# A two-layer gated cross-attention kernel: loops written out, and the attention tail through queries by heads

## The chip, the core and the metric

The kernel runs on one core of one Trainium2 chip. The metric is the device time in microseconds of one execution, as the median of several. TensorE is called PE here (PEld for its weight loads), VectorE DVE, ScalarE ACT, GpSimd POOL, SyncE SP.

## The reference

Eight sequences of 100 tokens with 128 features pass two layers. Each layer has a gated cross-attention over 1444 context tokens of the same sequence, and a gated mixture of experts. Everything is float32. Cut to what matters here:

```python
# x (8, 100, 128), ctx (8, 1444, 128); 16 heads of 8
q = (layernorm(x) @ Wq + bq).reshape(B, S, H, D).transpose(0, 2, 1, 3)      # k, v the same from ctx
scores = einsum('bhqd,bhkd->bhqk', q, k) / sqrt(D)      # layer 0: where(mask, scores, lowest)
attention = softmax(scores, axis=-1)                    # layer 1: then times a gate of each key
out = einsum('bhqk,bhkd->bhqd', attention, v).transpose(0, 2, 1, 3).reshape(B, S, 128)
x = x + tanh(g_xattn[l]) * (out @ Wo + bo)
x = x + tanh(g_ffn[l]) * experts(layernorm(x))          # 64 experts + a shared one; 8 experts of 352
```

## The kernel before

The program is written per engine, and the order of each engine's instructions is fixed by hand; semaphores join the engines. It runs attention(0), experts(0), attention(1), experts(1) on all of them.

**Attention.** The eight sequences are the batches b. A batch is worked in 12 slots t, one for each tile of 121 keys. In slot t PE computes the scores of that tile for all 16 heads in four matmuls (g = 0 to 3) of 128x400, L1156 (in layer 0 each followed by the mask's matmul L1159); ACT takes the exponent of two groups at a time, L851; PE weighs the values with the exponents of the tile before, 16 small matmuls for each half, L1177, into the bank `po`. The rows of `po` are 32 to a head of a group (8 weighted values, then the sum of the exponents, then unused ones), its columns 4 groups by 100 queries.

Beside this, the slots of batch b prepare batch b + 1: its keys (L1086), its values (L1103), its queries stacked by head (POOL), and the maximum of the scores over all keys, which is to be subtracted. For that PE multiplies queries with keys in blocks ("chunks", L1129; 48 a batch in layer 0, 39 in layer 1), and DVE reduces each to one column (L417 with the mask in layer 0, L420 in layer 1). `MAX_PER_SLOT` tells how many chunks fall in a slot, and the constants `SCORES_TIME` to `TURN_TIME` after which of PE's steps in the slot each is issued. A chunk may not start before DVE has taken the one two before. At a batch's end DVE makes the row maxima (L427, L430), PE turns them (L1137), and DVE writes them into the stacked queries (L438), for which the next batch's scores wait.

**The tail of a batch** turns `po` into the attention's output. It lies in the slots of the following batch. In slot 0 ACT copies `po` to `oraw` (L879). In slot 3 (`DEN_SLOT`) PE spreads each head's sum over its 32 rows with the constant `den_sel` (`den`, L1195). In slots 3, 4, 5 and 6 DVE takes the reciprocal of one group of 100 columns each (`reciprocals`, L448), and behind the last multiplies `oraw` by them (`normalise`, L453). In slot 7 (`OUT_SLOT`) PE projects (`project`, L1201): four matmuls, one for each group, with a `wo` whose rows are spread to match (128 x 4 x 128, 256 KB a layer). Then DVE adds the bias, applies the gate and adds to the residual (`add_out`, L458, L461, L465). All of PE's results of the tail, and those for keys and values, share one bank, `pc`. The tail of batch 7 has no slots to lie in: it follows the stage, its four reciprocals one behind the other. Before it, the tail of batch 6 lies in the slots of batch 7, where DVE also normalises the tokens of batches 0 to 5 for the experts (`layer_norm`), splits them (`split_tokens`) and, in layer 0, begins the routing (`route0`).

**Loops.** Batches 1 to 6 are a hardware loop on each engine, three passes of two batches (SP has a similar one); batches 0 and 7 are written out. Inside, the batch number is in a register: thresholds of waits and some addresses are worked out from it.

**Experts.** 33 units of weights in layer 0 and 22 in layer 1. For each unit PE runs 12 matmuls (gate and up, `gate_up`) and 6 (down, `down`), all in L1294; ACT, DVE and POOL work between them (L928, L537, L775, L938, L528). Most units are in loops, four to a pass. At the end PE turns the sum with eight transposes (L1343).

## Time and profile before

| | us |
|---|---|
| median of 3 runs | 1180.16 |
| lowest, highest | 1178.17, 1180.94 |
| the profiled execution | 1175.95 |
| its span, first to last instruction | 1174.2 |

| engine | busy us | share |
|---|---|---|
| PE | 1022.6 | 87% |
| PEld | 715.6 | 61% |
| DVE | 853.9 | 73% |
| ACT | 543.2 | 46% |
| POOL | 349.4 | 30% |

The granted clock of TensorE averages 0.911 of full speed. The attention of layer 0 takes the span to about 500 us, its experts to 655, the attention of layer 1 to about 1040, its experts the rest. The rows quoted below come from the profiled page and from questions to the trace of the same execution. "issue" is time in which an engine waited for nothing that the profile shows. A letter q behind an engine's name is its sequencer.

### The profile page before, as it was taken

How to read it: one execution, taken by the hardware profiler on the slowest of the kernel's cores; microseconds unless marked ns; L12 is line 12 of the kernel's file. 1: busy time of each engine (PE TensorE's matmuls, PEld its weight loads, DVE VectorE, ACT ScalarE, POOL GpSimd, SP SyncE). 2: the span in 40 equal slices, each digit the busy share in tenths (PEclk: the TensorE clock that was granted, in tenths of full speed). 3: DMA queues.
4: the chain of work that ended last, by engine and by line, in shares of the span. 5: the costliest groups of instructions: out<-in, count | busy, mean ns of one | idle time of the engine just before them, and what ended most of it. 6: DMA issues, size and time to landing. Idle time of an engine off the chain costs nothing.

```text
span 1174.2 us, 27964 instructions
## 1 busy us (share of the span) xinstructions
PE 1022.6 (87%) x9788; PEld 715.6 (61%) x9788; DVE 853.9 (73%) x1943; ACT 543.2 (46%) x810; POOL 349.4 (30%) x278
## 2 busy tenths in 40 slices
PE   4889999799979999958999689999899899861997
PEld 2356666566656666647888446666566566541886
DVE  7977777667767776667999787778678578540896
ACT  2033534343434445625666315555555455640664
POOL 6522121212121201005777441242142241000674
PEclk8589999999989999968999959999899899975899
DMA  7531303030303040008554323414304304004662
GB/s 182 98 68 36 77 27 78 28 77 27 77 28 77 2 104 1 2 11 235 165 166 137 66 77 81 99 31 100 78 27 91 80 11 104 3 1 66 180 166 69
DMA packets 48235, 89.05 MB, mean 76 GB/s; under 512 B 21170, under 2 KB 31446, under 8 KB 48118
## 3 DMA queue, kind: packets, MB, share of 16 engines
q1 hardware_dynamic: 48118, 87.42, 30.6%
q8 instruction: 82, 1.34, 0.5%
q14 instruction: 35, 0.29, 0.1%
HBM read 47.70 MB, written 1.75 MB: 42 GB/s over the span
## 4 chain that ended last, share of the span: by engine, by line
PE 71%; DVE 12%; issue 8%; ACT 2%; POOL 1%; DVEq 0%; ACTq 0%; POOLq 0%
PE pm L1129 16%; PE po L1177 14%; PE ps L1156 12%; PE ps L1294 8%; PE ps L1159 6%; PE pm L1294 4%; PE pc L1086 4%; PE pc L1103 3%; DVE mx_part L420 2%; DVE qsel L528 2%; DVE negm L430 2%; PE pc L1201 1%; PE pc L1195 1%; DVE qst L438 1%; POOL tmpf L775 1%
## 5 line engine op out<-in xcount | busy, mean ns | idle before, releaser
L851 ACT ACTIVATE probs<-ps 121x800 f32<-121x800 f32 (+1 forms) x384 | 321.3, 838 | 339.9 <-PE ps L1159 216.3
L1129 PE MATMUL pm<-khi,qbd 128*100 128x482 f32 (+5 forms) x653 | 317.9, 498 | 12.8 <-DVE mx_part L417 9.7
L417 DVE CUSTOM_DVE_ANT_0 junk<-pm,negq 100x482 bf16<-100x482 f32 (+1 forms) x360 | 229.5, 654 | 76.4 <-PE pm L1129 58.8
L1156 PE MATMUL ps<-qst,kst 128*121 128x400 f32 (+1 forms) x768 | 263.8, 409 | 19.7 <-issue 13.8
L420 DVE TENSOR_REDUCE mx_part<-pm 128x1 f32<-128x482 f32 (+3 forms) x293 | 183.6, 650 | 49.7 <-PE pm L1129 49.6
L1177 PE MATMUL po<-probs,vaug 121*32 121x100 f32 x6144 | 216.0, 259 | 3.9 <-ACT oraw L879 3.6
L1177 PEld LDWEIGHTS po<-probs,vaug 121*32 121x32 f32 x6144 | 129.8, 111 | 118.3 <-issue 105.0
L1156 PEld LDWEIGHTS ps<-qst,kst 128*121 128x121 f32 (+1 forms) x768 | 142.3, 189 | 60.6 <-issue 40.9
L1129 PEld LDWEIGHTS pm<-khi,qbd 128*100 128x100 f32 (+2 forms) x653 | 115.2, 178 | 89.2 <-issue 36.6
L1294 PE MATMUL ps<-qsel,qst 128*128 128x400 f32 x660 | 140.6, 365 | 1.1 <-DVE qst L520 1.1
L775 POOL TENSOR_TENSOR tmpf<-vaug,wb 128x400 f32<-128x400 f32 x55 | 67.1, 1220 | 220.3 <-DMA wb<-routing 160.6
L1159 PE MATMUL ps<-negT,ident_b 121*121 121x400 bf16 (+1 forms) x384 | 132.2, 344 | 0.0
L1294 PEld LDWEIGHTS ps<-qsel,qst 128*128 128x128 f32 x660 | 129.5, 202 | 3.2 <-DVE qsel L572 1.4
L1294 PE MATMUL pm<-qsel,qst 128*128 128x400 f32 x330 | 84.4, 369 | 37.2 <-DVE qsel L528 34.0
L718 POOL TENSOR_TENSOR vaug<-vraw,bv 121x512 f32<-121x512 f32 x24 | 31.8, 1328 | 269.4 <-ACT vraw L872 269.4
L528 DVE TENSOR_TENSOR qsel<-tmpf,qsel 128x400 fp32r<-128x400 f32 x55 | 60.8, 1105 | 50.3 <-ACT qsel L938 50.3
L1294 PEld LDWEIGHTS pm<-qsel,qst 128*128 128x128 f32 x330 | 58.0, 193 | 55.7 <-DVE qsel L528 55.2
L718 POOL TENSOR_TENSOR vraw<-vraw,bv 121x512 f32<-121x512 f32 x24 | 31.1, 1298 | 190.7 <-ACT vraw L872 190.7
L702 POOL TENSOR_TENSOR qst<-qsel,head_mask 96x400 fp32r<-96x400 f32 x64 | 52.5, 850 | 85.2 <-PE po L1177 73.9
L775 POOL TENSOR_TENSOR t<-vaug,wb 128x400 f32<-128x400 f32 x55 | 72.9, 1325 | 0.5 <-DVE vaug L537 0.5
L938 ACT CAST qsel<-tmpf 128x400 fp32r<-128x400 f32 x55 | 29.0, 527 | 88.8 <-POOL tmpf L775 88.8
L402 DVE SCALAR_TENSOR_TENSOR klo<-pc,bk,khi 128x482 fp32r<-128x482 f32 (+1 forms) x42 | 30.0, 714 | 55.0 <-ACT khi L863 55.0
(176 smaller groups left out, 1109.8 us busy)
## 6 DMA issues: line engine op xcount, KB each, us to landing
kst<-khi SPq DMA_DIRECT2D x128, 180.5 KB, 3.8
wb<-routing SPq DMA_DIRECT2D x66, 200.0 KB, 3.5
ctxT<-in_ctxT SPq DMA_DIRECT2D x16, 722.0 KB, 4.4
kst<-klo SPq DMA_DIRECT2D x64, 180.5 KB, 3.9
wts<-in_experts SPq DMA_DIRECT2D x55, 192.0 KB, 3.4
wb<-routing SPq DMA_DIRECT2D x22, 400.0 KB, 4.0
qsel<-qhi SPq DMA_DIRECT2D x16, 100.0 KB, 2.4
routing<-vaug SPq DMA_DIRECT2D x1, 1100.0 KB
```

The costliest lines, as they stand in the source:

```text
L417: ins = nc.vector.tensor_tensor_reduce(junk[:, k % 2, 0:w], max_bank(b, k)[0:S, 0:w], negq[:, lo:lo + w], 1.0, -3e38, ALU.add, ALU.max, mx ...
L420: ins = nc.vector.tensor_reduce(mx_part[0:rows, i, c:c + 1], max_bank(b, k)[0:rows, 0:w], AX, ALU.max)
L528: nc.vector.tensor_tensor(h_lo[v], hw[v], h_hi[v], ALU.subtract).then_inc(m["h_low"], 1)
L702: nc.gpsimd.tensor_tensor(qst[par][0:96, g * GQ:(g + 1) * GQ].rearrange("p (j q) -> p j q", q=S), qsel[0:96, g, bass.ds(b * S, S)].unsquee ...
L718: nc.gpsimd.tensor_tensor(raw4 if l else dst, raw4, bias, ALU.add).then_inc(s["v_written"], 1)
L775: nc.gpsimd.tensor_tensor(hw[v], tu[v], wb[slot][:, v * HALF:(v + 1) * HALF], ALU.mult).then_inc(m["weighted"], 1)
L851: nc.scalar.activation(probs[t % 2][0:r, 2 * u * GQ:2 * (u + 1) * GQ].rearrange("p (g q) -> p g q", q=GQ), ps[0:r, 2 * u:2 * u + 2, 0:GQ], ...
L1129: nc.tensor.matmul(max_bank(b, k)[0:rows, 0:w], qbd[:, first:first + rows], khi[:, lo:lo + w], start=True, stop=True).then_inc(s["chunk_re ...
L1156: mm = nc.tensor.matmul(ps[0:r, g, 0:GQ], kst[par][:, g, t * KEY_TILE:t * KEY_TILE + r], qst[par][:, g * GQ:(g + 1) * GQ], start=True, sto ...
L1159: mm = nc.tensor.matmul(ps[0:r, g, 0:GQ].rearrange("p (j q) -> p j q", q=S), ident_b[0:r, 0:r], negT[0:r, t, :].unsqueeze(1).broadcast_to( ...
L1177: mm = nc.tensor.matmul(po[32 * j:32 * j + 32, g * S:(g + 1) * S], vaug[par][0:r, t, 9 * h:9 * h + 32], probs[t % 2][0:r, h * S:(h + 1) * ...
L1294: mm = nc.tensor.matmul(dst, w, x, start=(alone and k == 0), stop=(alone and k == 2), skip_group_check=not alone)
```

## The change

Two things are changed together.

1. Every hardware loop, on all five engines and in attention and experts, becomes a loop of the program that builds the kernel, so that its passes are written out one behind the other with constants in place of registers. They are DVE L495 and L552, POOL L760 and L780, ACT L908 and L953, PE L1278 and L1328, SP L1458 and L1510, all changed in the same way; the diff shows some of them.
2. The tail. In slot 3 PE turns `oraw` with four transposes, so that `pc` has the queries as rows and, as columns, 16 heads of 32. DVE then takes one reciprocal of 100x16 and multiplies, which gives 100x128 (`normalise`, both in slot 3). In slot 5 (`BACK_SLOT`) PE turns that back (`turn_back`) and DVE copies it out (`take_back`). In slot 7 PE projects with one matmul against the plain 128x128 `wo`. `den_sel` is no longer loaded, and `wo` has 64 KB a layer. The constants that place the chunks follow. On DVE, behind `layer_norm` of the stage's end, `take_back(6)` stands between `normalise(6)` and `split_tokens`.

```diff
@@ -77,14 +77,13 @@
 V_SLOTS = [8, 9, 10]
 
 
-DEN_SLOT, OUT_SLOT = 3, 7
-RECIPROCAL_SLOTS = {3: [0], 4: [1], 5: [2], 6: [3]}
+DEN_SLOT, BACK_SLOT, OUT_SLOT = 3, 5, 7
 
 
 BESIDE_AFTER = {1: 1, 2: 1, DEN_SLOT: 2}
 
 
-SCORES_TIME, WEIGH_TIME, K_TIME, V_TIME, DEN_TIME, OUT_TIME, TURN_TIME = (34, 17), 30, 80, 100, 67, 100, 10
+SCORES_TIME, WEIGH_TIME, K_TIME, V_TIME, DEN_TIME, BACK_TIME, OUT_TIME, TURN_TIME = (34, 17), 30, 80, 100, 40, 10, 25, 10
 
 
 NEGM_WRITES = [[(J * g, J * g + J, S) for g in range(G)], [(0, 4, 128), (4, 7, 128), (7, 10, 128), (10, 12, 128),
...
@@ -92,8 +91,8 @@
 
 IN_FLIGHT, IN_FLIGHT_FIRST = 2, 4
 
-TAIL = G + 3
-OUT_TAKEN = G + 1
+TAIL = 4
+OUT_TAKEN = 2
 
 
 PARTS = {"a": (0, 6), "b": (6, 8)}
...
@@ -152,7 +150,7 @@
         wq = [sb(f"wq{l}", [128, 128]) for l in range(2)]
         wk = [sb(f"wk{l}", [128, 128]) for l in range(2)]
         wv = [sb(f"wv{l}", [128, 128]) for l in range(2)]
-        wo = [sb(f"wo{l}", [128, G, 128]) for l in range(2)]
+        wo = [sb(f"wo{l}", [128, 128]) for l in range(2)]
         bq = [sb(f"bq{l}", [128, 1]) for l in range(2)]
         bk = [sb(f"bk{l}", [128, 1]) for l in range(2)]
         bv = [sb(f"bv{l}", [128, 128]) for l in range(2)]
...
@@ -199,8 +197,9 @@
         junk = sb("junk", [100, 2, 512], BF16)
         probs = [sb(f"probs{i}", [KEY_TILE, HQ]) for i in range(2)]
         oraw = sb("oraw", [128, GQ])
-        rden = sb("rden", [128, GQ])
-        onorm = sb("onorm", [128, GQ])
+        rden = sb("rden", [100, H])
+        onorm = sb("onorm", [100, D])
+        onormT = sb("onormT", [128, S])
 
 
         tmpf = sb("tmpf", [128, NKP])
...
@@ -441,20 +440,24 @@
                                                 max_mask[96:128, lo:hi].unsqueeze(2).broadcast_to([32, hi - lo, w]),
                                                 ALU.mult).then_inc(s["negm_ready"], 1)
 
-                def reciprocals(b, g):
-                    cols = slice(g * S, (g + 1) * S)
-
-                    dve.wait_ge(s["tail_ready"], 2 * b + 1)
-                    nc.vector.reciprocal(rden[:, cols], pc[:, cols]).then_inc(s["tail_step"], 1)
-
                 def normalise(b):
-                    dve.wait_ge(s["tail_step"], b * TAIL + G)
-                    dve.wait_ge(s["oraw_ready"], b + 1)
-                    nc.vector.tensor_tensor(onorm[:], oraw[:], rden[:], ALU.mult).then_inc(s["onorm_ready"], 1)
+
+                    turned = pc[0:S, :].rearrange("q (h e) -> q h e", e=32)
+                    dve.wait_ge(s["tail_ready"], 3 * b + 1)
+                    nc.vector.reciprocal(rden[:].unsqueeze(2), turned[:, :, DH:DH + 1]).then_inc(s["tail_step"], 1)
+                    dve.wait_ge(s["tail_step"], b * TAIL + 1)
+                    nc.vector.tensor_tensor(onorm[:].rearrange("q (h d) -> q h d", d=DH), turned[:, :, 0:DH],
+                                            rden[:].unsqueeze(2).broadcast_to([S, H, DH]), ALU.mult)\
+                        .then_inc(s["onorm_ready"], 1)
+
+                def take_back(b):
+
+                    dve.wait_ge(s["tail_ready"], 3 * b + 2)
+                    nc.vector.tensor_copy(onormT[:], pc[:, 0:S]).then_inc(s["onormT_ready"], 1)
 
                 def add_out(b):
 
-                    dve.wait_ge(s["tail_ready"], 2 * b + 2)
+                    dve.wait_ge(s["tail_ready"], 3 * b + 3)
                     nc.vector.tensor_tensor(t2[0:S, 0:D], pc[0:S, 0:D], bo[l][0:S, :], ALU.add)\
                         .then_inc(s["tail_step"], 1)
                     dve.wait_ge(s["tail_step"], b * TAIL + OUT_TAKEN)
...
@@ -469,9 +472,10 @@
 
                     if main and 0 < t < 3:
                         k_low(b + 1, t)
-                    if tail:
-                        for g in RECIPROCAL_SLOTS.get(t, []):
-                            reciprocals(b - 1, g)
+                    if tail and t == DEN_SLOT:
+                        normalise(b - 1)
+                    if tail and t == BACK_SLOT:
+                        take_back(b - 1)
 
                 def slots(b, main, tail, par):
 
...
@@ -482,8 +486,6 @@
                             chunk_max(b + 1, k)
                             if i == BESIDE_AFTER.get(t, 0):
                                 beside(b, t, main, tail)
-                            if tail and t == max(RECIPROCAL_SLOTS) and i == 1:
-                                normalise(b - 1)
                         if tail and t == OUT_SLOT:
                             add_out(b - 1)
                     row_max(b + 1, 1 - par)
...
@@ -492,14 +494,13 @@
                 slots(0, True, False, 0)
                 if l == 0:
                     energy_gates()
-                with dve.Fori(0, (B - 2) // 2) as i:
+                for i in range((B - 2) // 2):
                     for k in range(2):
                         slots(i * 2 + (1 + k), True, True, 1 - k)
 
                 layer_norm(2 * l + 1, "a")
-                for g in range(G):
-                    reciprocals(B - 2, g)
                 normalise(B - 2)
+                take_back(B - 2)
 
                 dve.wait_ge(s["vproj_done"], V_CHUNKS * B)
                 dve.wait_ge(s["qstack_ready"], G * B)
...
@@ -508,9 +509,8 @@
                 if l == 0:
                     route0("a")
                 add_out(B - 2)
-                for g in range(G):
-                    reciprocals(B - 1, g)
                 normalise(B - 1)
+                take_back(B - 1)
                 add_out(B - 1)
                 dve.wait_ge(s["tail_step"], TAIL * B)
 
...
@@ -757,7 +757,7 @@
                     nc.gpsimd.tensor_tensor(negT[:], negT[:], any_b[0:KEY_TILE, :].unsqueeze(1)
                                             .broadcast_to([KEY_TILE, KEY_TILES, S]), ALU.mult).then_inc(pool_init, 1)
                 prep(1, 1)
-                with pool.Fori(0, (B - 2) // 2) as i:
+                for i in range((B - 2) // 2):
                     for k in range(2):
                         prep(i * 2 + (2 + k), k)
 
...
@@ -1192,15 +1192,18 @@
                     else:
                         pe.wait_ge(s["negm_ready"], (b + 2) * len(NEGM_WRITES[l]))
                     pe.wait_ge(s["oraw_ready"], b + 1)
-                    nc.tensor.matmul(pc[:, 0:GQ], den_sel[:], oraw[:], start=True, stop=True)\
+                    for g in range(G):
+                        mm = nc.tensor.transpose(pc[0:S, g * 128:(g + 1) * 128], oraw[:, g * S:(g + 1) * S], ident[:])
+                    mm.then_inc(s["tail_ready"], 1)
+
+                def turn_back(b):
+                    pe.wait_ge(s["onorm_ready"], b + 1)
+                    nc.tensor.transpose(pc[:, 0:S], onorm[:], ident[0:S, 0:S]).then_inc(s["tail_ready"], 1)
+
+                def project(b):
+                    pe.wait_ge(s["onormT_ready"], b + 1)
+                    nc.tensor.matmul(pc[0:S, 0:D], onormT[:], wo[l][:], start=True, stop=True)\
                         .then_inc(s["tail_ready"], 1)
-
-                def project(b):
-                    pe.wait_ge(s["onorm_ready"], b + 1)
-                    for g in range(G):
-                        mm = nc.tensor.matmul(pc[0:S, 0:D], onorm[:, g * S:(g + 1) * S], wo[l][:, g, :],
-                                              start=(g == 0), stop=(g == G - 1))
-                    mm.then_inc(s["tail_ready"], 1)
 
                 def slots(b, main, after, prep, par):
 
...
@@ -1248,6 +1252,9 @@
                         if spreads:
                             den(b - 1, prep)
                             maxima(DEN_TIME)
+                        if turns_back:
+                            turn_back(b - 1)
+                            maxima(BACK_TIME)
                         if projects_out:
                             project(b - 1)
                             maxima(OUT_TIME)
...
@@ -1275,13 +1282,14 @@
 
                 slots(-1, False, False, True, 1)
                 slots(0, True, False, True, 0)
-                with pe.Fori(0, (B - 2) // 2) as i:
+                for i in range((B - 2) // 2):
                     for k in range(2):
                         slots(i * 2 + (1 + k), True, True, True, 1 - k)
                 slots(B - 1, True, True, False, 1)
                 for u in range(2):
                     weigh(B - 1, KEY_TILES - 1, u, 1)
                 den(B - 1, False)
+                turn_back(B - 1)
                 project(B - 1)
 
             def experts(l, opening=False):
...
@@ -1556,9 +1563,7 @@
             w = {n: m.T for n, m in w.items()}
         b = {n: i[f"L{l}_xattn_b{n}"] for n in "qkvo"}
         a[f"wq{l}"], a[f"wk{l}"], a[f"wv{l}"] = w["q"], w["k"], w["v"]
-        wo = np.zeros((J, 32, G, D), f)
-        wo[:, 0:DH] = w["o"].reshape(G, J, DH, D).transpose(1, 2, 0, 3)
-        a[f"wo{l}"] = wo.reshape(128, G, D)
+        a[f"wo{l}"] = w["o"]
         a[f"bq{l}"], a[f"bk{l}"] = b["q"][:, None], b["k"][:, None]
         a[f"bv{l}"], a[f"bo{l}"] = np.broadcast_to(b["v"], (128, 128)), np.broadcast_to(b["o"], (128, 128))
     a["wr0"], a["wr1"] = i["L0_ffn_gate_weight"].T, i["L1_ffn_router_w"].T
```

## Rows read from the trace of the kernel before

**Rows 1.** The page, section 4: the chain that ended last, by engine.

```profile
PE 71%; DVE 12%; issue 8%; ACT 2%; POOL 1%; DVEq 0%; ACTq 0%; POOLq 0%
```

**Rows 2.** Stretches from L1137 to L1137: length, busy (instructions) by engine, PEclk, DMA.

```profile
171.28:228.20 56.92, 54.05 (x569) 35.74 (x569) 40.59 (x113) 24.11 (x31) 10.00 (x8) 0.94 0.23 54
228.20:288.60 60.40, 54.29 (x569) 35.74 (x569) 40.42 (x113) 24.22 (x31) 9.99 (x8) 0.92 0.22 51
288.60:344.19 55.59, 52.70 (x569) 34.91 (x570) 40.57 (x113) 24.12 (x31) 10.01 (x8) 0.97 0.23 55
344.19:404.52 60.33, 54.34 (x569) 35.85 (x569) 40.42 (x113) 24.23 (x31) 10.00 (x8) 0.92 0.18 39
404.52:456.80 52.28, 51.15 (x569) 34.23 (x570) 38.83 (x113) 23.85 (x31) 7.12 (x7) 1.00 0.25 59
820.85:868.12 47.27, 42.46 (x513) 28.09 (x513) 32.82 (x57) 23.94 (x31) 13.08 (x12) 0.93 0.27 62
868.12:910.82 42.70, 40.88 (x513) 27.29 (x513) 32.92 (x57) 23.95 (x31) 13.07 (x12) 1.00 0.30 72
910.82:958.75 47.93, 43.12 (x513) 28.45 (x513) 32.82 (x57) 24.13 (x31) 13.08 (x12) 0.93 0.23 49
```

**Rows 3.** The chain that ended last, 228 to 236 us: start, length, what.

```profile
230.72 2.70 issue
```

**Rows 4.** Waits of PE: for what, us in total, times, longest.

```profile
PE ps L1156 <- issue: 13.8, 4, 3.9
```

**Rows 5.** The chain again, 600 to 620 us, layer 0's experts.

```profile
602.57 2.21 PE ps L1294 x12
...
617.10 2.20 PE ps L1294 x12
```

**Rows 6.** Stretches: slots 3, 7 of batch 0; 3, 4-6, 7 of batch 4.

```profile
77.66:81.24 3.58, 3.58 (x45) 2.41 (x44) 2.87 (x9) 1.83 (x3) 0.00 (x0) 1.00 0.71 155
92.06:96.14 4.08, 4.07 (x46) 2.54 (x45) 3.25 (x11) 1.67 (x2) 0.00 (x0) 1.00 0.00 0
304.33:308.63 4.30, 4.30 (x47) 2.81 (x46) 3.14 (x11) 1.67 (x3) 0.00 (x0) 1.00 0.73 150
308.63:319.46 10.83, 10.83 (x133) 7.24 (x132) 9.63 (x28) 5.19 (x7) 0.00 (x0) 1.00 0.68 147
319.46:324.48 5.02, 5.00 (x54) 3.44 (x53) 3.64 (x12) 1.68 (x2) 0.00 (x0) 1.00 0.00 2
```

**Rows 7.** The chain over the span: L1195 and L1201 in both layers.

```profile
305.90 0.87 PE pc L1195 x2
321.11 1.05 PE pc L1201 x8
...
942.16 0.87 PE pc L1201 x8
```

**Rows 8.** The chain over the span: transposes behind the experts.

```profile
653.81 1.08 PE ps L1343 x8
```

**Rows 9.** DVE in order of time: start, length, what, tiles, shapes.

```profile
496.79 0.29 DVE L458 TENSOR_TENSOR t<-pc,bo 100x128 f32<-100x128 f32 x1
```

**Rows 10.** Stretches of the last tail of each layer, columns as in rows 2.

```profile
498.00:504.37 6.37, 2.94 (x10) 1.96 (x10) 3.27 (x5) 1.16 (x1) 0.00 (x0) 0.82 0.01 3
1036.61:1042.57 5.96, 2.52 (x10) 1.54 (x10) 3.27 (x6) 1.16 (x1) 0.00 (x0) 0.90 0.00 0
```

**Rows 11.** Line L1343: ns least/median/most, first and last start.

```profile
L1343 PE MATMUL ps<-ident,vaug x16: 272/272/316, 653.8 to 1168.5; 128*100 128x128 f32 x16
```

**Rows 12.** Groups of DVE: busy us, mean ns | idle before, releaser.

```profile
L448 DVE RECIPROCAL rden<-pc 128x100 f32<-128x100 f32 x64 | 48.0, 765 | 21.2 <-PE pc L1195 21.2
...
L458 DVE TENSOR_TENSOR t<-pc,bo 100x128 f32<-100x128 f32 x16 | 4.6, 285 | 9.1 <-PE pc L1201 9.0
```

**Rows 13.** Line L604 alone, columns as in rows 11.

```profile
L604 DVE RECIPROCAL rsum<-rsum x1: 202/202/202, 518.6 to 518.6; 100x8 f32<-100x8 f32 x1
```

**Rows 14.** The page, section 3: a DMA queue, packets, MB, share.

```profile
q8 instruction: 82, 1.34, 0.5%
```

More of the change, by code:

```diff
@@ L114 @@
 CONSTS_EARLY = ["wk0", "bk0", "wv0", "ident", "wq0", "bq0", "head16_mask"]
-CONSTS_LATE = ["head_mask", "bv0", "max_mask", "den_sel", "gates", "wo0", "bo0", "before", "tie_mask", "wr0", "ebias",
+CONSTS_LATE = ["head_mask", "bv0", "max_mask", "gates", "wo0", "bo0", "before", "tie_mask", "wr0", "ebias",
                "wk1", "bk1", "wv1", "wq1", "bq1", "bv1", "wo1", "bo1", "wr1"]
@@ L142, in flamingo @@
         max_mask = sb("max_mask", [128, H])
-        den_sel = sb("den_sel", [128, 128])
         before = sb("before", [100, S])
@@ L281, in flamingo @@
             "khi_ready", "klo_ready", "vraw_ready", "v_written", "qstack_ready", "qbd_ready", "negm_ready",
-            "maxrow_ready", "kproj_done", "vproj_done", "onorm_ready", "tail_step", "rowmax_step", "chunk_seen")) for l in range(2)]
+            "maxrow_ready", "kproj_done", "vproj_done", "onorm_ready", "onormT_ready", "tail_step", "rowmax_step", "chunk_seen")) for l in range(2)]
         for l in range(2):
@@ L551, in experts @@
                 unit(1, 1)
-                with dve.Fori(0, (units - 4) // RING) as i:
+                for i in range((units - 4) // RING):
                     for k in range(RING):
@@ L779, in experts @@
                 weigh(0, 0)
-                with pool.Fori(0, (units - 1) // RING) as i:
+                for i in range((units - 1) // RING):
                     for k in range(RING):
@@ L907, in attention @@
                     step(nc.scalar.activation(egate[:], egate[:], ACT.Exp, scale=-1.0), "energy_exp")
-                with act.Fori(0, (B - 2) // 2) as i:
+                for i in range((B - 2) // 2):
                     for k in range(2):
@@ L952, in experts @@
                 unit(1, 1)
-                with act.Fori(0, (units - 4) // RING) as i:
+                for i in range((units - 4) // RING):
                     for k in range(RING):
@@ L1212, in slots @@
                         spreads = after and t == DEN_SLOT
+                        turns_back = after and t == BACK_SLOT
                         projects_out = after and t == OUT_SLOT
@@ L1215, in slots @@
                         whole = (main * G * SCORES_TIME[l] + weighs * 2 * WEIGH_TIME + projects_k * K_TIME
-                                 + projects_v * V_TIME + spreads * DEN_TIME + projects_out * OUT_TIME
+                                 + projects_v * V_TIME + spreads * DEN_TIME + turns_back * BACK_TIME + projects_out * OUT_TIME
                                  + turns_maxima * TURN_TIME)
@@ L1277, in attention @@
                 slots(0, True, False, True, 0)
-                with pe.Fori(0, (B - 2) // 2) as i:
+                for i in range((B - 2) // 2):
                     for k in range(2):
@@ L1327, in experts @@
                                      skip_group_check=True)
-                with pe.Fori(0, (units - 1) // RING) as i:
+                for i in range((units - 1) // RING):
                     for k in range(RING):
@@ L1415, in stack @@
                                      part[32 * g:32 * g + 32, :].bitcast(F32)).then_inc(s["kstack_in"][par], 16)
-            tile_of = dict(ident=ident, head_mask=head_mask, head16_mask=head16_mask, max_mask=max_mask, den_sel=den_sel,
+            tile_of = dict(ident=ident, head_mask=head_mask, head16_mask=head16_mask, max_mask=max_mask,
                            before=before, tie_mask=tie_mask, gates=gates, wr0=wr0, wr1=wr1, ebias=ebias)
@@ L1457, in attention @@
                 context(l, 3, 1)
-                with sp.Fori(0, (B - 4) // 2) as i:
+                for i in range((B - 4) // 2):
                     for k in range(2):
@@ L1509, in experts @@
                     context(1, 1, 1)
-                with sp.Fori(0, (units - RING) // RING) as i:
+                for i in range((units - RING) // RING):
                     for k in range(RING):
@@ L1546 @@
     a["max_mask"] = (row[:, None] - 96 == np.arange(H)).astype(f)
-    a["den_sel"] = (row[:, None] == row // 32 * 32 + DH).astype(f)
     a["before"] = (row[:S, None] < row[:S]).astype(f)
```

## Prediction, on record before the kernel ran

> **What bounds the kernel now.** First I read the chain that ended last, by engine: PE holds 71% of it, DVE 12% [rows 1]. So what is taken off DVE alone is worth nothing in most stretches, and what is taken off PE, or lets PE start again earlier, is worth its full length. Next, the attention stages batch by batch, cut where PE turns the row maxima (L1137), the last step of a batch's preparation [rows 2]. In layer 0 the stretches take 56.92, 60.40, 55.59, 60.33 and 52.28 us, in layer 1 47.27, 42.70 and 47.93. The reader is to see a pattern of two: the long ones lie where a loop body of two batches ends and jumps back (two such jumps in each layer, since each loop runs three times; its last pass falls through). Their granted clock is lower too (0.92 against 0.97; 0.93 against 1.00).
>
> The chain at one of these jumps shows what happens [rows 3]: DVE writes the last negated maxima until 230.72, and then nothing that the profile knows of holds PE back, yet its next matmul starts only 2.70 us later, "issue". The waits of PE list exactly four such stalls before L1156, 13.8 us, the longest 3.9 [rows 4]. At the other batch ends L1156 has none. The experts' loops jump back too, but there the chain keeps its step: from 602.57 to 617.10 are four units, 3.63 us each, which is one whole pass and so holds one jump [rows 5]. Their body is much shorter (36 PE instructions a unit by the code; an attention batch has over a thousand, weight loads counted [rows 2]).
>
> **Loops written out.** The same work is issued in the same order; the jumps, the counters and the register arithmetic for waits and addresses go. In layer 0 I compare 60.40 and 60.33 with 55.59: 4.8 + 4.7 = 9.5 us. In layer 1 47.27 and 47.93 with 42.70: 4.6 + 5.2 = 9.8 us. That is more than the bare stalls, because matmuls behind a stall run at 1.2 GHz for a while; in layer 1 the other batch ends show no fall of the clock at all [rows 2]. Sum 19.3 us. The bounds come from the neighbours: against 56.92, the worst ordinary stretch, layer 0 gives 6.9 instead of 9.5; against 52.28, plus some 1.7 us that its end lacks (there GpSimd prepares no further batch), 12.7. So 16.7 to 22.5. In the experts' loops: 0 [rows 5]. For the register arithmetic 0 as well: slots of batch 0, which is already written out, and of batches inside the loop differ only where the tail has work [rows 6].
>
> **The tail inside the stream (slots 3 to 7 of the following batch).** PE now spends 0.87 us on the denominators (two passes of 400 columns) and 1.05 us on the projection (four matmuls, eight instructions), 0.87 in layer 1, where I take 0.87 for the denominators too [rows 7]. The slots confirm it: slot 3 takes 4.30 us with the denominators and 3.58 without, slot 7 5.02 with the projection and 4.08 without [rows 6], so 0.72 + 0.94 = 1.66 of the 1.92 reach the slot lengths; the rest lies in slack that the slots have anyhow. Added are four transposes with 128 moving columns, one transpose back with 128, and one matmul of the projection's old form. Eight such transposes at the end of an expert stage take 1.08 us, so 0.135 each [rows 8]. New: 4 x 0.135 + 0.135 + 1.05/4 = 0.94 us, in layer 1 0.68 + 0.87/4 = 0.90. By the chain's rows a tail saves 1.92 - 0.94 = 0.98 and 1.74 - 0.90 = 0.84; since a quarter of a microsecond of the old cost was slack, I take 0.9 and 0.8. Seven tails a layer lie in the stream. The seventh of layer 0 counts only 0.3: its batch ends in DVE's routing work, whose last piece and the three additions behind it (from 496.79 on) come just before the last denominators at 498.00 [rows 9, 10], so DVE is next there. Sum: 6 x 0.9 + 0.3 + 7 x 0.8 = 11.3 us. Lower bound: a transpose's own duration, 0.272 us [rows 11], as if nothing of it overlapped: 5 x 0.272 + 0.26 = 1.62, saving 0.3 or less, 4 us in all; upper bound the chain's 0.98 and 0.84, about 12.
>
> The Trainium skill (TensorE: Matmul & The Clock Gate, Part 4: PE-mode transpose) gives about 275 ns for a transpose in a kernel's context. That speaks against this change: five a tail would cost 1.4 us and the sum would lose some 10 us. The durations here agree with it (272 ns), but the starts stand half as far apart.
>
> DVE loses four reciprocals of 0.765 us and the 128x400 product, and gets a reciprocal of 16 columns, a product and a copy of 100x128 out of PSUM. By 0.202 us for 8 columns and 0.765 for 100, 16 columns take about 0.25; the product 0.285 as L458, and the copy no more [rows 12, 13]. So the 3.1 us of the reciprocals alone become 0.8. I cost that gain at nothing inside the stream: slots 4 to 6, where three of the reciprocals stand, take 10.83 us in batch 4, 3.61 each, what slot 3 with as many maxima takes in batch 0 with none (3.58), and in slots 3 and 7 PE is busy throughout [rows 6]. The new waits: PE waits in slot 5 for DVE's product of slot 3, two slots old. DVE waits in slot 5, behind its first chunk maximum, for the transpose back; PE issues that right behind the slot's first weighing, so under 0.3 us, and behind it in DVE's queue stand chunk maxima with two banks in flight. PE waits in slot 7 for DVE's copy of slot 5. At the end of the stage take_back of batch 6 stands ahead of split_tokens in DVE's queue; it delays that by less than 1 us, and nobody needs the split tokens before the stage is over.
>
> **The last tail, with nothing beside it.** From the last denominators to the first addition behind the projection, 6.37 us pass in layer 0 and 5.96 in layer 1 [rows 10]. New: four transposes 0.65 until readable (0.135 x 3 + 0.27), reciprocal 0.25, product 0.29, transpose back 0.3, copy 0.26, projection 0.5, and some 0.2 of handovers: 2.45 us. Saved 3.9 + 3.5 = 7.4 us; with each piece a quarter longer 6.2. What follows is serial (norm, routing, weights by way of DRAM), so it all moves forward.
>
> **The constants.** One load of 64 KB goes and two of 256 KB become 64 KB; attention's first work waits on DVE by then. 0.
>
> **Sum.** 19.3 + 11.3 + 7.4 = 38.0 us. The profiled execution took 1175.95 us (span 1174.2), so it would become 1138; the median of the runs is 4.2 above it, so I forecast 1142.
>
> **Rivals.** (a) Tails bring nothing in the stream: transposes cost their full duration, or PE finds DVE 0.8 us late in slot 5 or 7. For it: a round trip more. Against: slack above. 1142 + 11 = 1153. (b) The stalls at the jumps cover another wait of the same length, which then shows (DVE's maxima, the stacked keys): only 18.7 us are gained, 1161. Against: four ordinary batch ends without one [rows 2]. (c) Slower: straight code starves. PE's instructions come as 82 packets of 16 KB over the run [rows 14], and the jump shows that a fetch not yet landed stops PE for 2.70 us [rows 3]. If every sequential fetch cost 1 us, 82 us come back: 1224; it decides from 38.0/82 = 0.46 us a fetch. Against: a pass of the loop crosses a dozen such fetches, and PE's waits list no stall inside one. The Trainium skill (Runtime: NRT & Kernel Launch, Instruction fetch mechanics) says that sequential fetching is mostly hidden and that a taken branch out of the fetched window is not; by that rule (c) fails, and the trace agrees. (d) The clock no longer falls at layer 0's batch ends either, as behind 404.52 (1.00 there) [rows 2]: up to 1.7 us for each of six ends and the larger of the bounds above, 1130.
>
> **How the numbers follow.** Forecast 0.72, (a) 0.10, (b) 0.07, (c) 0.03, (d) 0.08. The low bounds give 16.7 + 4 + 6.2 = 26.9, 1153; the high ones 22.5 + 12 + 7.8 = 42.3, 1138, and (d) reaches 1130. With a spread of some 2 us between runs: 1130 to 1156. A difference of 0.2% (2.4 us) is about what can be told from none. Faster 0.96 (all but (c) and a hundredth), same 0.01, slower 0.03.
>
> **What would show it.** Right: batch stretches of layer 1 all at 41.5 to 42.2 us, of layer 0 all between 52 and 56; no "issue" wait before the scores' first matmul; slot 3 near 4.0, slot 7 near 4.2 in layer 0; the last tail near 2.5 us. Wrong: "issue" gaps at even distances in PE (c), a wait of L1137's kind at the places of the old jumps (b), transposes 0.27 us apart or PE waiting for the copy (a).

## The result, and the profile after

The changed kernel takes **1135.3 us** (median of 4 runs, 1133.09 to 1137.42) against 1180.55 for the kernel before (4 runs, 1178.17 to 1183.35): a ratio of 0.9616, with a 95% interval of 0.9587 to 0.9644, so 45.3 us are gained (42 to 49). The forecast was 1142 (1130 to 1156). The profiled execution took 1135.48 us with a span of 1133.7, which is 40.5 us below the profiled execution of before. By the medians the gap is larger, because that execution of before stood 4 to 5 us below its own median, and the one of after stands at its own median.

First the chain that ended last, by engine, in the kernel after.

```profile
PE 56%; DVE 18%; issue 6%; POOL 6%; ACT 4%; DMA 4%; SPq 1%; DVEq 0%; POOLq 0%; ACTq 0%
```

PE is still the first name on it, with less than the 71% of [rows 1]. Then the stretches from L1137 to L1137, columns as in [rows 2]: batches 1 to 6 of layer 0, then three of layer 1.

```profile
115.61:169.69 54.08, 51.47 (x566) 34.37 (x566) 41.72 (x116) 24.20 (x32) 10.00 (x8) 0.97 0.24 56
169.69:223.85 54.16, 51.53 (x567) 34.54 (x568) 38.71 (x111) 24.24 (x31) 10.00 (x8) 0.97 0.24 56
223.85:278.03 54.18, 51.57 (x567) 34.49 (x568) 38.77 (x111) 24.25 (x31) 10.00 (x8) 0.97 0.24 57
278.03:330.65 52.62, 50.00 (x566) 33.66 (x566) 38.71 (x111) 24.25 (x31) 10.00 (x8) 1.00 0.24 58
330.65:384.76 54.11, 51.50 (x566) 34.38 (x567) 38.61 (x111) 24.25 (x31) 9.99 (x8) 0.97 0.20 43
384.76:437.24 52.48, 51.49 (x566) 34.54 (x567) 37.06 (x111) 24.05 (x31) 7.12 (x7) 0.97 0.25 59
717.01:758.60 41.59, 40.03 (x510) 26.65 (x510) 30.80 (x55) 24.04 (x31) 13.11 (x12) 1.00 0.30 73
758.60:800.19 41.59, 40.05 (x510) 26.66 (x511) 30.79 (x55) 24.04 (x31) 13.09 (x12) 1.00 0.31 73
841.77:883.35 41.58, 40.06 (x510) 26.67 (x511) 30.80 (x55) 24.03 (x31) 13.10 (x12) 1.00 0.31 71
```

The pattern of two in [rows 2] is gone. Layer 1 runs at 41.58 or 41.59 in every batch, with the granted clock at 1.00. In layer 0 the stretches of 60 us have gone, but most still show 0.97. The waits of PE (for what, us in total, times, longest) tell the same.

```profile
PE pm L1302 <- DVE qsel L528: 36.4, 5, 26.4
PE pc L1137 <- DVE negm L429: 22.2, 16, 3.0
...
PE pc L1196 <- DVE xres L468: 1.1, 1, 1.1
...
PE ps L1156 <- issue: 0.6, 4, 0.2
```

The four stalls of 13.8 us in [rows 4] are down to 0.6 us. In their place nothing new of that size stands; the wait for the negated maxima (L429, one in each batch) was there before, with 24.4 us.

**The tail in the stream.** Slot 3, slots 4 to 6 and slot 7 of batch 4 in layer 0, columns as in [rows 6].

```profile
291.98:295.98 4.00, 4.00 (x49) 2.81 (x50) 2.88 (x10) 1.89 (x3) 0.00 (x0) 1.00 0.67 139
295.98:306.87 10.89, 10.89 (x134) 7.32 (x135) 8.56 (x28) 5.05 (x7) 0.00 (x0) 1.00 0.71 154
306.87:310.95 4.08, 4.08 (x48) 2.79 (x49) 3.28 (x11) 1.71 (x3) 0.00 (x0) 1.00 0.01 4
```

Against 4.30, 10.83 and 5.02 in [rows 6] that is 1.18 us less. Slot 7 now has the very length that it has in batch 0 with no tail at all.

**The last tail.** The chain of layer 0 (start, length, what), and then the stretch of layer 1's last tail with its columns.

```profile
479.46 0.66 PE pc L1196 x4
480.12 0.02 issue
480.14 0.27 DVE rden L447
...
480.43 0.30 DVE onorm L449
...
480.78 0.32 PE pc L1201
...
481.12 0.27 DVE onormT L456
...
481.44 0.76 PE pc L1205 x2
482.20 0.02 issue
482.22 0.30 DVE t L461
```

```profile
1000.76:1003.21 2.45, 1.38 (x7) 0.75 (x7) 0.81 (x3) 1.16 (x1) 0.00 (x0) 1.00 0.00 0
```

From the first transpose to the first addition 2.76 us pass in layer 0 and 2.45 in layer 1, where [rows 10] had 6.37 and 5.96. In layer 0 the projection runs at a granted clock of 0.50 and takes 0.76 us, against 0.48 in layer 1.

**Where the 40.5 us of the two profiled executions lie**, by the starts of L1137 and of the last denominators in each trace. The seven stretches of layer 0 before its last batch: 393.9 to 374.4, 19.5 less. Its last batch: 41.2 to 42.2, 1.0 more. Its last tail: 3.6 less. From there to the first L1137 of layer 1 (routing, experts, norms), in which nothing but loops was changed: 190.7 to 193.6, 2.8 more. Layer 1's seven stretches: 306.3 to 290.7, 15.6 less; its last batch 0.9 less, its last tail 3.5 less, the rest 1.2 less. The 2.8 are no loss by the change: the first four kernels below take 194.6 to 195.7 us for the same part, with and without loops in it, so the profiled execution of before was a quick one there. The growth of layer 0's last batch isn't one either: its slot 2 took 3.87 us at a granted clock of 0.67 here and 2.77 at 1.00 before, and in the last kernel below, which has the same tail, it takes 2.76.

### The profile page after: what moved, and what is told of

It is laid out like the page before. It is cut to its first block, busy times and chain, and to the rows that moved or that the text cites. A ratio compares the mean times of both kernels' runs of the same rounds, so it can differ in the third digit from the quotient of the medians.

```text
span 1133.7 us, 24532 instructions
## 1 busy us (share of the span) xinstructions
PE 998.4 (88%) x9740; PEld 702.5 (62%) x9740; DVE 820.9 (72%) x1911; ACT 543.7 (48%) x810; POOL 351.3 (31%) x278
## 4 chain that ended last, share of the span: by engine, by line
PE 56%; DVE 18%; issue 6%; POOL 6%; ACT 4%; DMA 4%; SPq 1%; DVEq 0%; POOLq 0%; ACTq 0%
PE pm L1129 15%; PE po L1177 13%; PE ps L1156 11%; POOL tmpf L775 6%; PE ps L1159 5%; PE pc L1086 4%; DVE junk L416 3%; PE pc L1103 3%; DVE vaug L537 3%; DVE qsel L528 2%; ACT qsel L938 2%; DVE mx_part L419 2%; DMA routing<-vaug 2%; DVE negm L429 2%; DVE qst L437 1%
## 5 line engine op out<-in xcount | busy, mean ns | idle before, releaser
L416 DVE CUSTOM_DVE_ANT_0 junk<-pm,negq 100x482 bf16<-100x482 f32 (+1 forms) x360 | 233.3, 657 | 78.8 <-PE pm L1129 57.9
L1156 PE MATMUL ps<-qst,kst 128*121 128x400 f32 (+1 forms) x768 | 260.3, 405 | 6.3 <-ACT probs L851 3.6
L419 DVE TENSOR_REDUCE mx_part<-pm 128x1 f32<-128x482 f32 (+3 forms) x293 | 186.0, 655 | 58.1 <-PE pm L1129 56.9
L1302 PE MATMUL ps<-qsel,qst 128*128 128x400 f32 x660 | 137.5, 359 | 1.1 <-DVE qst L520 1.1
L1302 PE MATMUL pm<-qsel,qst 128*128 128x400 f32 x330 | 84.6, 369 | 40.5 <-DVE qsel L528 36.4
L702 POOL TENSOR_TENSOR qst<-qsel,head_mask 96x400 fp32r<-96x400 f32 x64 | 52.6, 853 | 62.0 <-PE po L1177 50.7
L537 DVE TENSOR_TENSOR vaug<-ps,tmpf 128x400 f32<-128x400 f32 x110 | 61.6, 561 | 1.1 <-PE ps L1302 0.9
```

Source lines behind the costliest of these rows:

```text
L416: ins = nc.vector.tensor_tensor_reduce(junk[:, k % 2, 0:w], max_bank(b, k)[0:S, 0:w], negq[:, lo:lo + w], 1.0, -3e38, ALU.add, ALU.max, mx ...
L419: ins = nc.vector.tensor_reduce(mx_part[0:rows, i, c:c + 1], max_bank(b, k)[0:rows, 0:w], AX, ALU.max)
L537: nc.vector.tensor_tensor(tu[v], ps[:, 2 + v, 0:HALF], sg[v], ALU.mult)\
L1156: mm = nc.tensor.matmul(ps[0:r, g, 0:GQ], kst[par][:, g, t * KEY_TILE:t * KEY_TILE + r], qst[par][:, g * GQ:(g + 1) * GQ], start=True, sto ...
L1302: mm = nc.tensor.matmul(dst, w, x, start=(alone and k == 0), stop=(alone and k == 2), skip_group_check=not alone)
```

## The experiments

The forecast's theory had three terms (jumps of PE 19.3, tails in the stream 11.3, last tails 7.4). Four kernels take the change apart, one puts DVE work back, two test the rule behind the jumps where none was seen, and one removes the wait that is left at the batch ends.

**All loops written out, the old tail kept.** The edit, for each of the ten loops:

```diff
-                with pe.Fori(0, (B - 2) // 2) as i:
+                for i in range((B - 2) // 2):
```

> The kernel before with all ten loops written out and its old tail. Theory A (PE's stalls at the four jumps and the low clock behind them are the loops' whole price, 19.3 us by the batch stretches): 1180.5 - 19.3 = 1161, ratio 0.984, and no issue wait before L1156. Theory B (the register arithmetic on DVE and PE costs as well, which would explain that the whole change brought some 45 us in the medians instead of 38): 1154 or less. Rival C (another wait of the same length stands behind the jumps): 1178 or more.

Measured: 1153.12 us (5 runs, 1151.66 to 1159.1) against 1179.56, ratio 0.9773 (0.9757 to 0.9789): 26.8 us, with 24.9 to 28.7 by the interval. The stalls are gone, and no wait took their place. That is 7.5 us more than the term of 19.3, and the interval leaves that number out; it is theory B's side. Two stretches of its layer 1:

```profile
731.55:773.72 42.17, 40.62 (x512) 27.26 (x513) 32.66 (x57) 24.01 (x31) 13.09 (x12) 1.00 0.31 72
773.72:815.92 42.20, 40.66 (x513) 27.29 (x514) 32.66 (x57) 24.01 (x31) 13.09 (x12) 1.00 0.31 71
```

The old tail is in them and no jump, and still they are 0.5 us shorter than the undisturbed 42.70 of [rows 2]. So something besides the jumps was cheaper too.

**The new tail alone, all loops kept.** The edit is the reverse of the one above, applied to the kernel after.

```diff
-                for i in range((B - 2) // 2):
+                with pe.Fori(0, (B - 2) // 2) as i:
```

> The changed kernel with its ten loops back: the new tail alone. Theory A (tails 11.3 us in the stream and 7.4 behind the stages, independent of the loops): 1180.5 - 18.7 = 1162, ratio 0.984. If the last tails alone count: 1173. By the profile after (slot 3 0.30 shorter, slot 7 0.95 shorter, slot 5 0.05 longer in layer 0; some 1.1 us a batch in layer 1) the stream gives 6 x 1.2 + 7 x 1.1 = 14.9 and the last tails 3.6 + 3.4: 1159. The four issue stalls must be back.

Measured: 1161.87 us (4 runs), ratio 0.984 (0.9819 to 0.986): 18.9 us (16.5 to 21.4), where 11.3 + 7.4 = 18.7 had been worked out. The stalls are back at full size:

```profile
PE ps L1156 <- issue: 14.8, 4, 4.4
```

With 26.8 from the loops alone that makes 45.7, against 45.3 for both together: the two halves of the change add up, within some 5 us that the three intervals leave open. Together with the waits listed in each trace, which show none in the place of the stalls, that speaks against another wait of the same length behind them.

**Only PE's attention loop written out.** One line of the ten:

```diff
@@ PE, attention
-                with pe.Fori(0, (B - 2) // 2) as i:
+                for i in range((B - 2) // 2):
```

> The kernel before with only PE's attention loop written out; nine loops stay. Theory A (it is PE that stands still at the jump, while DVE, ACT, POOL and SP have slack there): the same 1161 as with all loops written out. Rival D (each engine's jump costs its share of the stall): between 1161 and 1178. DVE's jump of that moment must then show a gap before its first maximum that PE waits for.

**The nine others written out, PE's attention loop kept.** Two of the nine:

```diff
@@ ACT, attention
-                with act.Fori(0, (B - 2) // 2) as i:
+                for i in range((B - 2) // 2):
...
@@ DVE, attention
-                with dve.Fori(0, (B - 2) // 2) as i:
+                for i in range((B - 2) // 2):
```

> The kernel before with nine loops written out and PE's attention loop left: the complement. Theory A: 1180, the same as before within 0.2%, four issue stalls of about 3.5 us before L1156. Rival D: 1163 to 1176.

Measured, on one chip: with PE's loop alone 1161.01 us (4 runs), ratio 0.9828 (0.9805 to 0.9852), 20.3 us less; with the nine others 1175.46 us (7 runs), ratio 0.9968 (0.995 to 0.9985), 4 us less (2 to 6). So the jumps of PE are worth what the stretches of [rows 2] had said, 19.3. The rest of the loops is not free, though: the nine others alone come out in the range of rival D (1163 to 1176), not at theory A's 1180. Two stretches with the nine written out, in layer 1, the first an ordinary one and the second with a jump of PE:

```profile
781.36:823.38 42.02, 40.71 (x513) 27.26 (x513) 32.63 (x57) 24.03 (x31) 13.10 (x12) 1.00 0.31 73
823.38:870.29 46.91, 41.97 (x512) 27.92 (x512) 32.63 (x57) 24.04 (x31) 13.09 (x12) 0.96 0.28 65
```

And one with PE's loop alone written out:

```profile
899.80:942.50 42.70, 40.73 (x512) 27.25 (x513) 32.81 (x57) 23.95 (x31) 13.11 (x12) 1.00 0.25 55
```

PE is busy for the same 40.7 us in both ordinary stretches; the one whose other engines have no loops is 0.68 us shorter. The longer one begins behind a jump of the other engines, but batch 1 of layer 1, with no jump of any engine in it, shows the same: 42.61 us with their loops and 42.03 without. So this part is not their jumps, as rival D has it, but what they do within a batch: with loops they work out wait values and addresses from registers. Measured from first score to first score in batch 1, slot 1, where PE waits for ACT's copy (L879), takes 4.50 us against 4.66, and slot 11, where PE waits for DVE's negated maxima, 2.89 against 3.30. Slot 8 is 0.18 shorter too, and no wait of PE is listed there, so that part is open. Over the whole run PE's wait before L1137 comes to 24.4 or 24.5 us in each of the three traces in which the other engines have attention loops and to 22.2 or 22.3 in those in which they have none: some 2 of the 4 us lie there.

The other engines' jumps do show once, in the kernel with PE's loop alone written out: PE waits 1.19 us at the batch end at 813.21 (0.87 at the end before), and the stretch behind it takes 43.77 us at a granted clock of 0.96, where its neighbours take 43.01 and 42.82.

**Four more reciprocals for DVE.** One 128x100 reciprocal, of the kind that the change removes, in each of the slots 3 to 6 of a batch with a tail (12 batches), into a tile that nobody reads:

```diff
+                    if tail and DEN_SLOT <= t < DEN_SLOT + G:
+                        nc.vector.reciprocal(rdum[:, (t - DEN_SLOT) * S:(t - DEN_SLOT + 1) * S], ones_f[:, 0:S])
```

> The changed kernel with four reciprocals of 128x100 (of a constant, into a tile that nobody reads) put back on DVE in slots 3 to 6 of each batch that has a tail, about 0.75 us each, 3 us a batch, 36 us in all (twelve such batches). Theory A (DVE has slack in those slots, its relief was worth nothing): the same as the changed kernel, 1135, within 3 us. Rival E (part of the stream's gain was DVE's relief, which would explain why slot 7 became 0.95 us shorter and not 0.8): 3 to 12 us longer, and slots 3 to 7 longer than 4.01, 3.61, 3.66, 3.60 and 4.08.

Measured: 1143.06 us (4 runs), ratio 0.9694 (0.9664 to 0.9724). That is 9 us above the kernel after by the ratios, 7.8 by the medians, so within rival E's 3 to 12. The same three stretches of batch 4 as above, and the chain in slot 4:

```profile
295.33:299.33 4.00, 4.00 (x50) 2.81 (x48) 2.88 (x9) 1.84 (x3) 0.00 (x0) 1.00 0.77 159
299.33:310.71 11.38, 11.01 (x134) 7.30 (x133) 10.47 (x32) 5.03 (x6) 0.00 (x0) 1.00 0.65 142
310.71:314.79 4.08, 4.08 (x48) 2.79 (x47) 3.28 (x11) 1.68 (x2) 0.00 (x0) 1.00 0.00 0
```

```profile
298.84 0.66 DVE junk L417
...
299.92 0.60 DVE rdum L479
...
300.60 0.60 DVE junk L417
...
301.26 0.47 PE pm L1132
```

Slots 3 and 7 keep their length; slot 4 loses 0.49 us, where DVE has the normalising of slot 3 behind it and the added reciprocal before the next chunk maximum, for which PE's L1132 waits. In the ordinary batches this comes to 0.5 us in layer 0 and 0.25 in layer 1; six of each make 4.5 us, and the other 3 to 5 lie outside those slots (in the profiled execution the stretches of layer 0 that the kernel after ran in 54.1 and 52.6 us all took 54.6). So DVE has less room in slot 4 than the forecast's "nothing" says, at least for a load of this kind. It doesn't show that the change gained from the relief there. In the kernel before, with the old reciprocals, those slots took 10.83 us and now take 10.89.

**A jump with a body of middle length.** [rows 5] showed no stall at the short jumps of the experts' loop. Here PE's experts' loop is kept, with passes of 16 units in layer 0 and 8 in layer 1: 576 and 288 PE instructions a pass, and one jump back in each layer.

```diff
+                per = (16, 8)[l]
-                for i in range((units - 1) // RING):
-                    for k in range(RING):
+                with pe.Fori(0, (units - 1) // per) as i:
+                    for k in range(per):
```

> The changed kernel with PE's experts' loop rolled again, but with long passes: two of 16 units in layer 0 (576 PE instructions a pass), two of 8 in layer 1 (288). Each layer jumps back once. Theory F (a jump costs only when its target is no longer held, which depends on the length of the body): no stall at either jump, units at 3.63 us throughout, 1135. Rival G (a jump costs whenever there was a fetch since the loop began): one issue gap of about 3 us in the middle of the experts of layer 0.

Measured: 1135.38 us in one run, profiled, with a span of 1133.4; the kernel after had 1135.48 and 1133.7. The units on either side of both jumps take 3.63 to 3.65 us, like all others. All that shows is one step: the second matmul behind the jump starts 0.28 and 0.22 us after the first, and 0.17 to 0.19 in the units beside it. The jump costs the run nothing that can be seen.

**A long body.** The same loops, with the gate product of each unit issued 5 times in layer 0 and 21 times in layer 1, so that a pass has 1344 and 2208 PE instructions. PE is then busy without a break, and a stall can't hide.

```diff
+                        for _ in range((3, 11)[l] * 2 - 2):
+                            product(ps[:, v, 0:HALF], w_hi[slot][:, 0, :], w_lo[slot][:, 0, :], x_hi[:, cols],
+                                    x_lo[:, cols], True)
```

> As the kernel with long passes, but with the gate's product repeated in each unit, five times in all in layer 0 and twenty-one in layer 1 (the last repetition counts, so the result is the same): passes of 1344 and 2208 PE instructions. It takes several hundred microseconds more, which says nothing; only the jumps count. Theory F with the attention's bodies in mind (about 2300 and 2050 PE instructions a pass, both stall): a stall of 2.7 to 3.5 us at the jump of layer 1, none or one at that of layer 0, depending on where between 576 and 2050 the limit lies. Rival H (the stall belongs to the attention's waits, not to the length): no stall at either.

Measured: 1708.93 us in one run; its total says nothing here, the places of the jumps do. By the count of matmuls, layer 0's jump lies at 629.20 (the chain merges it into the pieces up to 629.36) and layer 1's at 1369.44. The chain at each:

```profile
621.71 6.55 PE ps L1302 x36
628.26 1.09 PE pm L1302 x6
629.36 6.55 PE ps L1302 x36
...
1368.73 0.71 issue
1369.44 15.62 PE ps L1302 x84
```

At the jump of 1344 instructions PE goes on without a gap. At the jump of 2208 there is an "issue" piece of 0.71 us, PE's starts stand 1.10 us apart (0.18 at the same place of the other units), and from one L928 on ACT to the next 26.22 us pass where 25.15 pass in the other units. The waits of PE put this gap down to DVE's L520, which ends 0.7 us before PE starts; but one unit earlier PE starts the same matmul at 1343.38, 0.2 us before that L520 ends, so it doesn't wait for it. Apart from the first and last units of each stage, where PE waits for DVE, no other place of the two stages has such a gap. So it is the length of the body that makes a jump expensive, not the jump: free up to 1344 instructions, not free at 2208, nor in attention at 1026 matmul and load instructions a batch, 2052 a pass, in layer 1 [rows 2]. The Trainium skill (Runtime: NRT & Kernel Launch, Instruction fetch mechanics) has the fetch exposed when the target of a taken branch is outside the window of fetched code. Its 2048 instructions for PE fit the two sides measured here. Its window of two pages of 256 instructions doesn't: the bodies of 576 and 1344 are longer than that and had no gap. What stays open is the price: an "issue" of 0.71 us here, where 2.7 to 3.5 were expected, against 2.70 at the jump of [rows 3]. Each of these two kernels ran once.

**The negation left out.** At each batch end PE waits for DVE to negate the reduced maxima. The mask with which L1137 multiplies them can carry the sign instead; what is computed stays the same.

```diff
-                    dve.wait_ge(s["rowmax_step"], b * 2 + 1)
-                    nc.vector.tensor_scalar(negm[0:rows, 96:96 + blocks], negm[0:rows, 96:96 + blocks], -1.0, None,
-                                            ALU.mult).then_inc(s["rowmax_step"], 1)
...
-                    pe.wait_ge(s["rowmax_step"], b * 2 + 2)
+                    pe.wait_ge(s["rowmax_step"], b + 1)
...
-    a["max_mask"] = (row[:, None] - 96 == np.arange(H)).astype(f)
+    a["max_mask"] = -(row[:, None] - 96 == np.arange(H)).astype(f)
```

> The changed kernel without L429 (the negation of the row maxima on DVE); max_mask holds -1 in place of 1, so that the product behind it negates. In the profile after, PE stands still 1.84 us at each batch end of layer 0 and 0.70 in layer 1, waiting for L429, which takes 1.82 us for 100x16 while POOL works on the next stacked queries, and 0.17 where POOL is idle. Theory I (the instruction waits for POOL, the reduction before it does not, and what follows reads one operand out of PSUM and does not either): layer 0 gains 7 x 1.84, layer 1 8 x 0.56, and the clock no longer falls at batch ends, some 1.7 us each for five: 17 to 26 us, 1109 to 1118. Rival J (the instruction behind it now waits for POOL in its place): 3 us at most, 1132.

Measured: **1111.65 us** (6 runs, 1109.28 to 1112.65), ratio 0.9423 (0.9401 to 0.9445) to the kernel before, some 23 us better than the kernel after. Its stretches, two of layer 0 and one of layer 1, and its chain at the batch end at 266.10 (the mask product is its L1133):

```profile
164.53:215.30 50.77, 49.98 (x568) 33.65 (x566) 36.91 (x110) 24.24 (x32) 9.99 (x9) 1.00 0.26 60
215.30:266.09 50.79, 50.01 (x569) 33.67 (x568) 36.95 (x110) 24.26 (x32) 10.00 (x9) 1.00 0.26 61
...
734.29:775.28 40.99, 39.99 (x510) 26.67 (x511) 30.25 (x54) 24.04 (x32) 13.10 (x12) 1.00 0.31 72
```

```profile
265.62 0.48 PE po L1173 x16
266.10 0.29 PE pc L1133
266.39 0.19 PE ps L1152
```

PE no longer waits at the batch end (0.12 us are left in layer 1), and layer 0's granted clock stays at 1.00 through its batches. Five of layer 0's six ordinary batches take 50.8 us, against 52.5 to 54.2 in the kernel after (the first takes 52.2: PE stands still for 1.25 us in it, until 0.1 us after ACT has written the next keys); layer 1's take 41.0 against 41.58. The 1.8 us of the wait and, where the clock fell, some 1.5 more per batch are what the tiny operation had cost. This is the version to keep.

## Why the prediction was right, point by point

- **What bounds the kernel** held: what was taken off PE, or let it start earlier, came back at full length.
- **The jumps of PE, 19.3.** Right in size and in place: 20.3 measured with that loop alone (17.5 to 23 by the interval). That they came from the body's length was an inference from one comparison; the two experiments with other bodies now bear it out, though at a smaller price for the one jump that stalled.
- **The register arithmetic, 0.** Mis-sized, and the step that failed. The forecast compared slots 3 to 7 of a batch written out with those of a batch in the loop [rows 6]. PE is busy throughout those, so other engines' overhead can't show there. It shows in slots 1 and 11, where PE waits for ACT and DVE: 0.15 us, and 0.1 to 0.4, in layer 1; 3.8 us over the run by the kernel with the nine others written out. In slot 11 it comes by way of GpSimd: the negation that PE waits for lasts 1.93 us in layer 0 and mostly 0.70 to 1.03 in layer 1 with loops, 1.82 and 0.54 without, and it ends with the GpSimd operation beside it (last section). The term for all loops came out at 26.8 instead of 19.3; 20.3 + 3.8 of the two partial kernels explain 24.1 of it. The other 2.7 are within their intervals; about 1 us of them can be seen, in the stretch of 43.77 us that the other engines' jump leaves behind when PE's is gone.
- **The tails in the stream, 11.3.** The sum is right by luck of two misses against each other. The forecast found a quarter of a microsecond of the old cost to be slack, which would have left 0.72 and 0.58 us a tail, and took 0.9 and 0.8 by judgement. In layer 0 a tail saves 1.18 us by the slots, not 0.9: the projection went from 0.94 to nothing in slot 7, where 4.2 was forecast and 4.08 came, so its one matmul lies in that slot's slack. In layer 1 it saves less than the 0.8: slot 3 went from 3.43 to 3.18, slot 7 from 3.84 to 3.39, and slot 5 rose by 0.11, so 0.6. That makes 6 x 1.18 + 7 x 0.6 = 11.3 before layer 0's seventh tail. That one was rightly held to be worth little: PE waits there for DVE's last addition (L468, 1.1 us), and no gain of that batch as a whole can be seen, since its length moved by more with the clock.
- **The price of a transpose, 0.135.** Right: four take 0.66 us on the chain until the last is readable, and one alone lasts 0.27, so they start 0.13 us apart. By the figure of the Trainium skill (TensorE: Matmul & The Clock Gate, Part 4: PE-mode transpose), taken for each of the five, the tail alone would have brought some 9 us, an estimate; it brought 18.9. One transpose lasts here what the page says (272 ns against about 275), so the figure is a duration and not a step.
- **The last tails, 7.4.** 3.6 + 3.5 = 7.1. Layer 1's 2.45 is the forecast; layer 0's 2.76 is longer because its projection ran at the low clock.
- **DVE's relief, nothing.** Nothing speaks against it (slots 4 to 6 are as long as before), but the reason given, that these slots have room, was too wide: four reciprocals put there on top of the new tail cost 8 to 9 us.
- **The rivals.** That the tails bring nothing, (a), fell to 18.9 us for the tail alone; another wait behind the jumps, (b), to the stretches and to the sum 26.8 + 18.9; starved straight-line code, (c), to the lack of any "issue" wait of PE above 0.2 us in the kernel after. Of (d), the clock that no longer falls in layer 0, one ordinary batch of the five shows it (278.03, at 52.62). The kernel without the negation shows it in all six, at 50.8 in five. The 1130 given for (d) is not its own sum: 1138 less six times 1.7 is 1128. The 7.8 in the high bound has no working either.
- **The sum.** 38.0 forecast, 45.3 measured by medians. Of the 7.3 missing, 7.5 are in the loops' term and 0.2 in the tail's, less 0.4 by which the two halves alone add up to more than both together. The high bounds of the terms end at 1138; that 1135.3 still lies in the range is luck, owed to the room left for (d), which hardly came, while no bound had priced the register arithmetic.

## What to carry to other kernels

Look at a loop's back jump on the engine that sets the pace: a body of some two thousand instructions stalled it at each pass (about 5 us in attention with the slow clock behind it, 1.1 in the experts), one of 1344 did not, so either write the loop out or keep its body short. What the other engines' loops do within a batch costs where the pacing engine waits for them, so look for it in the slots with a wait and not in the full ones. And a tiny operation at the end of a reduction can be the dearest of the stage: fold its sign or scale into a constant that is multiplied anyway.

## What the runs showed of the hardware that was not expected

The negation of a 100x16 tile on DVE lasts ten times as long at six batch ends of layer 0 as at the seventh. Line L429 in layer 0 of the kernel after (ns least/median/most, first and last start, shapes), and who waited for it:

```profile
L429 DVE TENSOR_SCALAR negm<-negm x7: 174/1818/1820, 113.7 to 437.0; 100x16 f32<-100x16 f32 x7
...
  PEld pc L1137: 12.8, 7
  PE pc L1137: 11.2, 7
```

The 174 ns is that at 437.0, the end of the batch before the last, where GpSimd has nothing more to prepare; at the others a GpSimd operation runs beside it. The same pair in the kernel before, in order of time (start, length, what, tiles, shapes):

```profile
225.26 2.86 POOL L691 TENSOR_TENSOR qbd<-qhi,head_mask 128x1600 fp32r<-128x1600 f32 x1 [0.75 <-PE pm L1129]
226.22 1.93 DVE L430 TENSOR_SCALAR negm<-negm 100x16 f32<-100x16 f32 x1
```

The GpSimd product ends at 228.12 and the negation at 228.15. So it is at 15 of the 16 batch ends in each of the nine traces that have the negation: it ends 0.03 us behind the GpSimd operation that was running when it began, whether that makes it 0.54, 0.70, 1.03, 1.17, 1.82 or 1.93 us long. The row maximum just before it (it writes the same tile, by a reduction) has no such spread, here in the kernel without the negation:

```profile
L426 DVE TENSOR_REDUCE negm<-mx_part x16: 195/200/204, 61.4 to 939.1; 100x16 f32<-100x48 f32 x8, 128x13 f32<-128x39 f32 x8
```

The 23 us of that kernel are the price of 16 such operations and of the clock that fell behind them. No run here takes the GpSimd work away; that GpSimd holds the operation up rests on the ends that coincide throughout, while the negation's start and the GpSimd operation beside it differ.

The second is how a jump's price depends on the length of the body, with nothing at 576 and 1344 instructions and a gap at 2208. The third is that the granted clock in layer 0 falls at some batch ends and not at others of like length: in the kernel after 0.97 in four of the five stretches from 115.61 to 384.76, 1.00 in one. It is not the batch: in the kernel whose experts' loop was kept, with the same attention, the stretches before it took 54.1 to 54.2 us and the one at 332.02 took 52.6, where the kernel after has 54.11. Why it spares one is open.
